# 128 bytes of SBUF left free below the sign bytes

## The reference

```python
out = lax.conv_general_dilated(x, weight, window_strides=(1,), padding=[(4, 4)],
                               dimension_numbers=('NCH', 'OIH', 'NCH'), feature_group_count=4)
out = out + ctx[:, :, None] + bias[None, :, None]
w = kernel.astype(x.dtype) * 2.0 - 1.0
x = x + scale * jnp.einsum('bsi,if->bsf', out, w)
```

## Time and profile before

| | us |
|---|---|
| median of the three runs | 175.43 |
| the three runs | 174.07, 175.43, 176.49 |
| the profiled execution's own time | 174.09 |
| its span | 172.2 |
| PE busy in it | 164.2 |
| DVE busy in it | 136.9 |

### The profile page before, as it was taken

The page is one execution under the profiler, slowest core; times in us unless marked ns, Lnnn a source line. Parts: engine busy times, 40 slices in busy tenths (PEclk is TensorE's granted clock), DMA queues, the critical chain, the costliest instruction groups (busy, mean ns, idle before and its releaser), DMA issues.

```text
span 172.2 us, 2765 instructions
## 1 busy us (share of the span) xinstructions
PE 164.2 (95%) x914; PEld 136.6 (79%) x914; DVE 136.9 (79%) x180; ACT 71.8 (42%) x68; POOL 37.6 (22%) x43
## 2 busy tenths in 40 slices
PE   7699999999999999999999999999999999999791
PEld 2378888998888779887998889887988899888580
DVE  4735493996999999779986899779977997699461
ACT  3201996470791148521781069304842340214000
POOL 4230600005040334006400343043400540000000
PEclk9969999999999999999999999999999999999999
DMA  5688697777799877887977888988888666414006
GB/s 205 139 159 248 249 196 196 125 200 188 143 337 237 256 153 306 184 229 189 297 185 176 262 173 306 225 249 112 331 214 204 94 249 138 105 49 199 0 0 244
DMA packets 27486, 33.38 MB, mean 194 GB/s; under 512 B 3537, under 2 KB 19857, under 8 KB 27473
## 3 DMA queue, kind: packets, MB, share of 16 engines
q1 hardware_dynamic: 22176, 25.63, 54.6%
q10 hardware_dynamic: 4912, 6.78, 14.8%
q0 software_dynamic: 384, 0.81, 2.2%
HBM read 10.06 MB, written 8.40 MB: 107 GB/s over the span
## 4 chain that ended last, share of the span: by engine, by line
PE 92%; DMA 3%; DVE 2%; issue 1%; ACTq 1%; DVEq 0%
PE ps_A L828 30%; PE ps_conv L809 18%; PE ps_C L828 15%; PE ps_conv L786 9%; PE ps_B L828 8%; DMA taps_nat<-weight 3%; PE ps_B L845 2%; PE ps_C L845 2%; PE ps_toep L845 2%; PE ps_A L845 2%; PE ps_toep L828 1%; PE ps_toep L765 1%; PE ps_C L776 1%; PE ps_A L753 1%; DVE sums L250 1%
## 5 line engine op out<-in xcount | busy, mean ns | idle before, releaser
L485 ACT CAST hi<-sums 128x1024 fp32r<-128x1024 f32 x14 | 14.7, 1049 | 44.5 <-DVE sums L622 38.4
L401 POOL TENSOR_TENSOR set<-x_blk 128x512 f32<-128x512 f32 x12 | 17.3, 1461 | 69.7 <-DMA x_blk<-x_phase 69.7
L643 DVE SCALAR_TENSOR_TENSOR x_nat<-ps_A,scale_col,x_nat 128x512 f32<-128x512 f32 x27 | 20.2, 748 | 15.0 <-PE ps_A L828 14.2
L442 ACT COPY x_phase<-x_nat 128x1032 f32<-128x1032 f32 x13 | 27.2, 2135 | 2.2 <-DMA x_nat<-x 2.2
L828 PE MATMUL ps_A<-sign_T,hi 128*128 128x512 f32 x80 | 22.4, 401 | 0.9 <-DVE x_nat L643 0.9
L485 ACT CAST hi<-y_sum 128x1024 fp32r<-128x1024 f32 (+1 forms) x14 | 11.7, 834 | 25.8 <-DMA y_sum<-y_two 16.5
L828 PE MATMUL ps_A<-sign_T,lo 128*128 128x512 f32 x80 | 22.0, 396 | 0.0
L828 PEld LDWEIGHTS ps_A<-sign_T,lo 128*128 128x128 f32 x80 | 15.0, 188 | 3.8 <-DVE lo L632 0.3
L828 PEld LDWEIGHTS ps_A<-sign_T,hi 128*128 128x128 f32 x80 | 14.5, 189 | 4.2 <-issue 1.3
L809 PE MATMUL ps_conv<-toeplitz,w_bytes 128*128 128x128 f32 x144 | 17.2, 276 | 0.4 <-DVE y_two L596 0.4
L809 PEld LDWEIGHTS ps_conv<-toeplitz,set 128*128 128x128 f32 x144 | 16.9, 192 | 0.8 <-issue 0.4
(11 more groups left out here) (108 smaller groups left out, 234.6 us busy)
## 6 DMA issues: line engine op xcount, KB each, us to landing
x_nat<-x SPq DMA_DIRECT2D x16, 512.0 KB, 4.4
out<-x_nat SPq DMA_DIRECT2D x15, 512.0 KB, 4.8
x_blk<-x_phase SPq DMA_DIRECT2D x118, 64.5 KB, 3.0
y_sum<-y_two ACTq DMA_DIRECT2D x48, 128.0 KB, 3.3
w_bytes<-w_bool SPq DMA_DIRECT2D x2, 512.0 KB, 6.5
shift<-shift_dram POOLq DMA_DIRECT2D x2, 256.0 KB, 4.2
x_blk<-x_phase ACTq DMA_DIRECT2D x6, 64.5 KB, 3.7
x_blk<-x_phase POOLq DMA_DIRECT2D x4, 64.5 KB, 3.0
```

The source lines that it names most:

```text
L401: nc.gpsimd.tensor_tensor(dif[r][:, e], x_blk[r][:, :, e:e + M:2], x_blk[r][:, :, e + 1:e + 1 + M:2][:, :, 0:K], ALU.subtract).then_inc(di ...
L442: nc.scalar.copy(x_phase[r][:, :, 0:M + 1], line(d, r, 0, PAD + L + PAD).rearrange("r (m q) -> r q m", q=B)).then_inc(phase_ok[r], B)
L485: nc.scalar.copy(parts(hi_all, k), group(k)).then_inc(hi_ok[k], 1)
L643: nc.vector.scalar_tensor_tensor(there, bank[b], scale2_col[:, :], there, ALU.mult, ALU.add).then_inc(summed[k], 1)
```

## The change

One tile of 32 float32 per partition is asked for between `ident` and `w_bytes`. Nothing reads or writes it. Every tile asked for after it lies 128 bytes higher in each partition: `w_bytes` with the view `set_1`, the seven sign tiles, `set_0`, `taps_nat`, `toeplitz`, and all the small tiles up to `scale2_col`. The tiles below, `hi`, `lo`, `x_blk`, `y_sum` and `x_nat` among them, stay where they are, and PSUM is not touched. No instruction is added, removed or moved.

```diff
         x_nat = sb("x_nat", [P, SLOTS, PAD + L + PAD])
 
         ident = sb("ident", [C, C])
+
+        offset = sb("offset", [P, 32])
         w_bytes = sb("w_bytes", [P, B, L], mybir.dt.uint8)
         signs = {k: sb(f"sign_{k}", [P, KH, BANK], F32R) for k in ("B11", "B21", "B22", "T1", "T2", "T3", "T4")}
```

## The result

The changed kernel takes 173.22 us against 175.16 us, medians of 22 runs each; the ratio is 0.988 with a 95% interval of 0.986 to 0.990. That is 1.2% faster: less than the 2% that the chances went by, with an interval clear of no change, and not the "nothing changes" of the forecast. 173.22 us lies inside the forecast's range of 173.0 to 177.5 us because that range was as wide as the spread of the runs, not because its mechanism held. The profiled executions are 169.7 and 172.2 us long.

A forecast was written before the change was run, and what follows sets the result against it. The prediction took TensorE to bound the kernel throughout; terms 0 + 0 + 0 + 0.1 us on the profiled 174.09 gave 174.2, and the 1.34 us offset to the median made 175.5 us, range 173.0 to 177.5 (8 in 10: 171.8 to 178.2).

The forecast's parts named there:

- the 2% that the chances went by: Whole kernel: 2% either way counts as no change; chances faster 0.13, same 0.77, slower 0.10.
- the "nothing changes" of the forecast: Whole kernel: no stage changes, 175.5 us; chance 0.68.
- What bounds the kernel.: Whole chain: TensorE bounds from start to end; from 45.6 to 161.6 us PE has 0.6 us of room.
- The open 16.7 ns of a product matmul: 448 product matmuls of 512 columns: 16.7 ns each left unexplained, 7.5 us of the kernel, possibly about addresses.
- Product matmuls: PE's product matmuls: distance between starts does not depend on position, 0 us; bounds -7.5 to +7.5 us.
- Rival A: Product matmuls: moving reads and next weight load stop meeting, the 16.7 ns stall goes, -7.5 us, 167.9 us; chance 0.13.
- Rival B: Product matmuls: the two reads start on the same position and meet, another 16.7 ns, +7.5 us, 183.0 us; chance 0.10.
- L809 and L786, DVE, ACT, POOL: Fast and early convolutions and the other engines: 0 us; POOL's 2.06 against 2.79 us pairs not due to position.
- DMAs into moved tiles, 0.1 us: Taps, shift, scale_col 0 us; sign bytes, without cover at B22, land later by 0 to 0.4 us, taken as 0.1.
- The rest of the sum: Whole kernel: 0 + 0 + 0 + 0.1 on the profiled 174.09 gives 174.2 us; with the 1.34 us offset, 175.5.

The follow-up runs named there:

- the 34 groups: Kernel before, plus 34 groups of 12 float32r matmuls behind its last sum, with block and moving-column starts varied; 226.7 to 235 ns a matmul at 512 columns.

## Why the prediction was wrong

- *What bounds the kernel.* Right. The product matmuls gave 2.4 of the 2.5 us between the two spans, at a granted clock of 1.00 in both; a stretch at 0.51 from 8.7 to 12.2 us is in both. That PE has 0.6 us of room came from its busy time, which hides the first part of every wait.
- *The open 16.7 ns of a product matmul.* Right that this was the number that a change of addresses could be about. It split into 5.3 ns that depend on the distance (232.6 to 227.3 in the kernel) and some 11 that none of the 34 groups moved; 226.7 is the least that was seen.
- *Product matmuls, "I take 0 us".* This is the step that failed, a term put at nothing. It measures 448 x 5.3 ns = 2.4 us, inside its bounds of 7.5 either way. Two arguments carried the zero. That distances in steps of 512 change nothing was true, and says nothing about 128. That steps of 32 change nothing was seen in the float32 convolutions and carried over to float32r products, which have another ratio of moving columns to loads; the convolutions indeed did not change (111.7 ns), the products did. I had written that distances which differ by 128 do not occur in products, and should have left the term open there.
- *A sign in the trace that I passed over.* The product matmuls had means from 392 to 404 ns for the same instruction, and in the single starts distances mostly from 228 to 241 ns, while the convolutions nearly all kept 111 or 112. I read that as small. In the changed kernel most of these groups have means of 389 or 390 ns and most distances are 226 or 227 ns.
- *Rival A.* Right in its place, its partner and its sign. Its size was three times too large, as it took all of the 16.7 ns. It had the geometry the wrong way round: it wanted the two starts to be separated modulo 256, and what helps is that they coincide to within 16 bytes. Rival B, the same meeting read the other way, had the picture of coinciding starts and the wrong sign.
- *L809 and L786, DVE, ACT, POOL.* Right: 111.7 ns, 1,215 and 1,217 ns, and POOL's differences 1,444 ns in the mean into `set_0` and 1,049 into `w_bytes`, where they took 1,461 and 1,050. The gap between the two, which the prediction left open, goes with DVE: in the changed kernel's trace a difference into `w_bytes`, with no addition of DVE's beside it, took 1.04 to 1.06 us, and most of those into `set_0`, with one beside it, 1.30 to 1.56.
- *DMAs into moved tiles, 0.1 us.* Not seen, and not excluded: the sign bytes landed in 6.3 us and ACT waited 0.15 us for them instead of 0.20. Over all kept traces they landed in 6.3 to 7.2 us where they start 128 bytes over a multiple of 256, and in 6.0 to 6.9 us where they start on one, so a difference of 0.1 us is lost in the spread. Whether the rule of the Trainium skill (DMA: Bandwidth & Descriptors, How a descriptor splits into AXI transactions), one transaction more for a start off a multiple of 256 bytes, holds on the side that is written can't be told from these runs.
- *The rest of the sum.* The matmuls gave 2.4 us and the medians 1.9. The profiled pair lost nothing, 2.5 us between its spans. An estimate from the waits at P1 (0.13 to 0.16 us more in each of up to four steps) and the 0.1 us that the wait in front of P3 grew by (0.26 to 0.37 us) is 0.1 to 0.7 us taken back in an execution. That this makes the difference of 0.5 us is argued and not shown: only one of the changed kernel's 22 executions has a trace here.

## What to carry to other kernels

Before costing a change of addresses at nothing, look at the distances between starts of identical matmuls: if they are longer than their columns explain, constant or not, measure a few placements with nothing else running; a dozen matmuls for each were enough here. For float32r matmuls of 512 columns with a new block each, give the stationary and the moving tile the same start modulo 256 (here 2.4 us of PE's time in a span of 172, and 1.9 us in the medians, for 128 unused bytes); with 256 columns it brought nothing. When the bounding engine gets faster, expect the neighbour with little room to take some of it back, and compare the same wait in several executions before blaming the change for it.

## What the runs showed of the hardware that was not expected

- For float32r at 512 columns, the time from start to start depends on where the moving columns start against the stationary block: 226.7 ns from start to start at distances of 240, 0 and 16 bytes modulo 256, 228.9 at 64, 230.0 at 80, and 232 to 235 elsewhere.
- The good distances make a constant row (226 or 227 ns). A bad one can make an irregular row (229 and 238 ns in turns at 128 bytes) or a nearly constant one (232 to 235 ns at 48), and a single good load between bad ones gains next to nothing (233.1 and 231.4 ns).
- Even the good distance leaves 13.3 ns over the 213.3 of 512 columns at 2.4 GHz; why was not tried.
- A DVE addition of two SBUF tiles takes 0.68 us or 1.53 to 1.54 us by who began first, DVE or POOL, some hundredths of a microsecond apart.
